# Squaring Q and K in four chunks instead of one piece, in an eight-core attention and FFN kernel

## What is computed

```python
h = layernorm(x)
Q, K, V = h @ Wq + bq, h @ Wk + bk, h @ Wv + bv          # 16 heads of 64
scores = Q K^T / sqrt(64) + mask                          # mask: -inf above the diagonal,
attn = softmax(scores)                                    #  -0.25 * log(distance) below it
x = x + (attn V) @ Wo + bo
h = layernorm(x);  hr, hi = split(h)
x = x + concat(hr Wr^T - hi Wi^T + br, hr Wi^T + hi Wr^T + bi)
```

## Time and profile before

| | us |
|---|---|
| median of 2 runs (range) | 1258.16 (1254.16 to 1262.17) |
| the profiled execution | 1259.46 |
| its span, slowest core (core 5) | 1257.9 |
| spans of the eight cores | 1235.4 to 1257.9 |
| prologue of Q, K squares on core 5 | 178.75 to 190.68 |
| attention on core 5 | 264 to 893 |

### The profile page before, as it was taken

How to read it: one execution, slowest core, us unless ns; L and a number is a source line. 1 busy time by engine, 2 the same in 40 slices (tenths; PEclk the granted TensorE clock), 3 DMA queues, 4 the chain that set the end, 5 groups by cost and what they waited for, 6 DMA issues and landing times.

```text
span 1257.9 us, 13946 instructions; the slowest of 8 cores (1235.4 to 1257.9 us)
## 1 busy us (share of the span) xinstructions
PE 767.4 (61%) x3672; PEld 263.0 (21%) x3672; DVE 603.2 (48%) x1163; ACT 451.8 (36%) x891; POOL 174.2 (14%) x132
## 2 busy tenths in 40 slices
PE   0001069695686766867669667766285746575556
PEld 0000024241221221312213122121021212121222
DVE  4555433247556475474664555545326342434342
ACT  0011010045765757667567576667300000000000
POOL 2212300014022040130350000000002010100000
PEclk9999998797796987879777789767666767768678
DMA  4111240424122031220310000000511011101101
GB/s 108 50 50 50 64 54 1 51 68 101 34 34 68 1 67 34 34 67 1 62 57 1 1 2 1 1 1 1 93 40 35 23 44 67 67 1 67 67 34 67
DMA packets 39394, 52.52 MB, mean 42 GB/s; under 512 B 21782, under 2 KB 23830, under 8 KB 39192
## 3 DMA queue, kind: packets, MB, share of 16 engines
q1 hardware_dynamic: 17944, 41.15, 9.9%
q0 software_dynamic: 21376, 10.49, 6.6%
HBM read 51.63 MB, written 8.39 MB: 48 GB/s over the span
## 4 chain that ended last, share of the span: by engine, by line
PE 47%; DVE 18%; DMA 10%; ACT 9%; issue 9%; DVEq 4%; POOL 2%; SPq 0%; ACTq 0%; POOLq 0%
PE qk L377 9%; DMA xrot<-x 7%; PE psF L938 7%; ACT PTb L630 6%; PE pv L677 6%; PE stP L605 5%; PE qk L480 5%; PE pr L692 4%; PE psW L871 4%; DVE PTb L654 3%; DVE PTb L649 3%; DVE stat L220 3%; DVEq L404 3%; POOL sqscr L218 2%; DVE stat L234 2%
## 5 line engine op out<-in xcount | busy, mean ns | idle before, releaser
L630 ACT ACTIVATE PTb<-stP,negCS 128x512 bf16<-128x512 f32 (+1 forms) x320 | 199.4, 623 | 243.8 <-PE stP L611 241.7
L649 DVE TENSOR_TENSOR PTb<-PTb,decayS 128x512 bf16<-128x512 bf16 (+1 forms) x320 | 147.0, 459 | 220.6 <-ACT PTb L630 213.4
L635 ACT ACTIVATE PTb<-stP,negCS 128x512 bf16<-128x512 f32 (+1 forms) x320 | 199.2, 622 | 0.0
L677 PE MATMUL pv<-PTb,V 128*64 128x512 bf16 (+1 forms) x320 | 138.0, 431 | 83.9 <-DVE PTb L654 78.5
L242 ACT ACTIVATE stat<-stat 128x1 f32<-128x1 f32 x32 | 6.5, 203 | 440.7 <-DVEq L237 440.6
L605 PE MATMUL stP<-QTs,KTs 64*128 64x512 bf16 (+1 forms) x320 | 133.2, 421 | 40.4 <-ACT PTb L635 40.4
L654 DVE TENSOR_TENSOR PTb<-PTb,decayS 128x512 bf16<-128x512 bf16 (+1 forms) x320 | 143.5, 448 | 16.4 <-ACT PTb L635 0.9
L685 PE MATMUL pv<-PTb,V 128*64 128x512 bf16 (+1 forms) x320 | 142.4, 445 | 0.0
L698 PE MATMUL pr<-PTb,ones 128*64 128x512 bf16 (+1 forms) x320 | 137.7, 432 | 0.0
L692 PE MATMUL pr<-PTb,ones 128*64 128x512 bf16 (+1 forms) x320 | 137.3, 431 | 0.0
L611 PE MATMUL stP<-QTs,KTs 64*128 64x512 bf16 (+1 forms) x320 | 133.8, 423 | 0.0
(11 more groups left out here) (91 smaller groups left out, 968.3 us busy)
## 6 DMA issues: line engine op xcount, KB each, us to landing
xrot<-x SPq DMA_DIRECT2D x28, 512.0 KB, 5.2
g1b<-g1rep SPq DMA_DIRECT2D x32, 256.0 KB, 2.6
g2b<-g2rep SPq DMA_DIRECT2D x32, 256.0 KB, 3.0
out<-outbuf SPq DMA_DIRECT2D x8, 1024.0 KB, 4.9
xrot<-x POOLq DMA_DIRECT2D x4, 512.0 KB, 4.3
Wqp<-wq POOLq DMA_DIRECT2D x8, 256.0 KB, 5.1
Wkp<-wk POOLq DMA_DIRECT2D x8, 256.0 KB, 6.8
WvS<-wv POOLq DMA_DIRECT2D x2, 1024.0 KB, 14.2
```

The source lines that it names most:

```text
L630: s.activation(PTb[:, slot * 1024 + no:slot * 1024 + 512], stP[j][:, no:512], AF.Exp, bias=negCS[:, pi:pi + 1]),
L635: s.activation(PTb[:, slot * 1024 + 512 + no:(slot + 1) * 1024], stP[j][:, 512 + no:1024], AF.Exp, bias=negCS[:, pi:pi + 1]),
L649: P.emit("vector", lambda v, slot=slot, off=off, no=no: v.tensor_mul(PTb[:, slot * 1024 + no:slot * 1024 + 512], PTb[:, slot * 1024 + no:s ...
L677: t.matmul(pv[0:64, no:512], V[:, mt * 1024 + h0 * 64:mt * 1024 + h0 * 64 + 64], PTb[:, slot * 1024 + no:slot * 1024 + 512], start=(mt == ...
```

## The change

Each square is cut into four of 512 columns, and each piece now stands directly in front of its own matmul and maximum, with a drain and a `yield` between square and matmul:

```diff
             for (kk, (which, srcT)) in enumerate((("q", QTs), ("k", KTs))):
-                P.emit("vector", lambda v, srcT=srcT, pi=pi: v.tensor_mul(
-                    qsqbf, srcT[:, pi * SEQ:(pi + 1) * SEQ],
-                    srcT[:, pi * SEQ:(pi + 1) * SEQ]),
-                    waits=[(aE, last_ev)])
-                sq = P.emit("vector", lambda v: v.drain(fusable=False), inc=vE)
-                yield
                 for c in range(NCH):
+                    P.emit("vector", lambda v, srcT=srcT, pi=pi, c=c: v.tensor_mul(
+                        qsqbf[:, c * 512:(c + 1) * 512],
+                        srcT[:, pi * SEQ + c * 512:pi * SEQ + (c + 1) * 512],
+                        srcT[:, pi * SEQ + c * 512:pi * SEQ + (c + 1) * 512]),
+                        waits=[(aE, last_ev)])
+                    sq = P.emit("vector", lambda v: v.drain(fusable=False), inc=vE)
+                    yield
                     j, pw = pool.acquire()
                     mm = P.emit("tensor", lambda t, j=j, c=c: t.matmul(
                         qkP[j][0:2, 0:512], hselS[:, :],
```

## The result

The changed kernel takes 1275.91 us (median of 11 runs, 1266.57 to 1288.77) against 1254.99 us before (10 runs). The ratio is 1.0153, 95% interval 1.0122 to 1.0185: slower by about 19 us. All ratios here, and the medians compared for n_before and n_after, leave out executions in the slower of the chip's two states. The forecast said 1270, +0.9%. The profiled execution took 1277.8 us. Its eight spans are longer than those of before by 24.0 us on average, the slowest one by 18.4.

What follows compares the result with a forecast made beforehand. Bound: inside a pair, a loop over PE, ACT and DVE with almost no slack. Prologue +7.7 and seven pairs +3.5 make +11.2 us on the profiled 1259.46; forecast 1270, +0.9%, range 1256 to 1286.

Steps and rivals of the forecast that it cites:

- the prologue: Before V: each cut square stands behind the previous chunk's maximum, so nothing overlaps: +7.7 us, ends +6.0 and +8.0.
- the pair's own term: Sum of the step terms in one pair, without POOL: taken as +0.5 us a pair, +3.5 us in seven.
- Steps 17 to 23: In a pair: three matmuls wait for fresh squares before attnV, 0.9 us each, +2.7 us; small chain leaves, -0.4.
- the small chain: Lines L418 to L438 in a pair: leaving steps 17 to 23 gives -0.4 us, coming to steps 25 to 28 costs 0 to +0.4.
- Steps 14 to 16: In a pair: the 2.77 us stall before K's first matmul goes; with earlier gains the pair stands at -2.7 us.
- Steps 24 to 28: End of the chunk in a pair: last matmul waits before attnV(23), +0.6 us; the small chain adds 0 to +0.4.
- POOL: In five pairs shorter but more squares meet POOL's work: bounds -0.5 to +1 us a pair, taken as 0.
- The signs: Expected in the profile: about 64 L409 waits, prologue 19 to 20 us, ACT idle about 2, every second exponential 3.9.
- A: Rival: waits with idle PE keep half clock until step 24: +3.2 us a pair, 1292 in all; chance 0.12.
- B: Rival: the clock recovers, the three attnV of step 16 run at 2.4 GHz: -1.5 us a pair, 1259; chance 0.17.
- C: Rival: the waits disappear and pairs come near pair 7's window: 49 us less in seven, 1218; chance 0.04.
- D: Rival: more short squares meet POOL: +1 us in five pairs, 1275; chance 0.67 together with the forecast.

Runs made afterwards that it cites:

- n_before: The kernel before without POOL's products, the FFN matrix set to zero once and not built: ratio 0.9761 to before, median 1223.9 us.
- n_after: The changed kernel without POOL's products, the FFN matrix set to zero once and not built: ratio 0.9891 to before, median 1242.6 us.
- e2: The kernel before with only the prologue's squares cut as in the changed kernel, the pairs keeping whole squares: ratio 1.0032.
- e1: The kernel before with only the pairs' squares cut as in the changed kernel, the prologue keeping whole squares: ratio 1.0124.
- e3: The pairs' squares cut as in the changed kernel, but each matmul three steps behind its square instead of one; prologue whole: ratio 0.9844 to before.
- e7: As e3, with cut squares in the pairs and a whole prologue, but each matmul two steps behind its square: ratio 0.9822 to before.
- e9: As e6, but each square in the pairs cut into four pieces with a drain each, all in one step: ratio 0.9937 to before.
- e6: The kernel before, whole squares, with one more empty step between each square and its first matmul: ratio 0.9785, 1229.56 us.
- e8: The kernel before, whole squares, with two more empty steps between each square and its first matmul where e6 has one: ratio 0.9861.

## Why the prediction was right, and where its sizes were off

The direction and the range held, and the mechanism was the one forecast: matmuls that wait for a square queued just behind the mask product. The size of the loss was 19 us for 11, and the two parts of the forecast were off by different amounts: the prologue was put a little too high (7.7 for 6.5 us), the pairs far too low (3.5 for 19.6). The pair's own +0.5 us was the small rest of large terms that nearly cancel, -2.7 and +2.7, so half a microsecond in any of them changes it as much as the term itself. By the prediction's own steps:

**The prologue.** Forecast +7.7 us with ends of 6.0 and 8.0; measured +6.5 in the trace, and e2 alone shows ratio 1.0032, 4 us with an interval that reaches to 8. The mechanism is as told. A chunk takes 2.09 us, not 2.19: from the start of a maximum to the end of the drain behind the next square it is 1.05 us (183.21 to 184.26 above), where I had put 0.69 + 0.03 + 0.43 = 1.15 and no overlap. The first two matmuls ran at the full clock (0.39 us).

**Steps 17 to 23.** Forecast +0.9 us for each of three waits, less 0.4 for the small chain. The exponentials of steps 17, 19, 21 and 23 start at 812.22, 816.18, 820.33 and 823.86 in pair 6 (core 3), 11.64 us in all; in the kernel before, at 790.79 and 800.10, it was 9.31. That is +2.3, as forecast, but core 3 is one of the two fortunate cores. Over the eight cores this stretch of pair 6 takes 12.3 us: 11.6 on the two with a clock of 0.98, 12.5 on the six with 0.84 or 0.85. So the forecast is right for the full clock, and the change costs up to 0.9 us more because the clock falls. The first wait, step 18, on core 3:

```profile
813.59 0.42 DVE L655 TENSOR_TENSOR PTb<-PTb,decayS 128x512 bf16<-128x512 bf16 x1
...
813.93 0.42 DVE L401 TENSOR_TENSOR qsqT<-KTs 128x512 bf16<-128x512 bf16 x1
...
814.77 0.38 PE L409 MATMUL qk<-qsqT,hselS 128*2 128x512 bf16 x1 [1.11 <-DVEq L406]
815.07 0.40 PE L678 MATMUL pv<-PTb,V 128*64 128x512 bf16 x1
...
816.18 0.69 ACT L631 ACTIVATE PTb<-stP,negCS 128x512 bf16<-128x512 f32 x1 [1.09 <-PE stP L612]
```

attnV starts 1.06 us after the mask product ended (814.01), where without the wait it is 0.14: the 0.92 that I had worked out. The same wait on core 0, where TensorE runs at the low level behind it:

```profile
812.68 0.43 DVE L655 TENSOR_TENSOR PTb<-PTb,decayS 128x512 bf16<-128x512 bf16 x1
...
813.86 0.59 PE L409 MATMUL qk<-qsqT,hselS 128*2 128x512 bf16 x1 [1.28 <-DVEq L406]
...
814.37 0.64 PE L678 MATMUL pv<-PTb,V 128*64 128x512 bf16 x1
...
816.13 0.69 ACT L631 ACTIVATE PTb<-stP,negCS 128x512 bf16<-128x512 f32 x1 [2.14 <-PE stP L612]
```

From the start of attnV to the exponential it takes 1.76 us here and 1.11 on core 3, and attnV itself starts 1.26 us after the mask product instead of 1.06. That it is the wait for a fresh square which costs most, and not the pieces, is shown by e1 against e3 and e7. The pieces are not free either: e9 against e6.

**Steps 14 to 16** were mis-sized. I let the pair stand at -2.7 us there; measured over eight cores it is -1.8 in pair 6 at the exponential of step 16 (against the kernel before, the intervals that start with the exponentials of steps 10, 11 and 15 are shorter by 0.80, 0.74 and 3.01 us, those of steps 12 and 14 longer by 0.91 and 1.85). The rows of core 3:

```profile
805.44 0.42 DVE L401 TENSOR_TENSOR qsqT<-QTs 128x512 bf16<-128x512 bf16 x1
...
806.24 0.59 PE L409 MATMUL qk<-qsqT,hselS 128*2 128x512 bf16 x1 [3.36 <-DVEq L406]
...
806.76 0.60 PE L606 MATMUL stP<-QTs,KTs 64*128 64x512 bf16 x1
...
807.30 0.63 PE L678 MATMUL pv<-PTb,V 128*64 128x512 bf16 x1
...
807.53 0.69 ACT L631 ACTIVATE PTb<-stP,negCS 128x512 bf16<-128x512 f32 x1 [1.73 <-PE stP L612]
```

PE was idle for 3.36 us in front of this matmul, more than the 2.77 of before: ACT was first busy with the reciprocals (802.08 to 803.49), and the square stands behind the mask product of step 13, whose exponentials came after them. It then ran at the half clock, so that ST(15) came 0.52 us later and attnV(12) 1.06, where I had put 0.3 and 0.5 by rows of the full clock, although showed the half clock at just this place.

**Steps 24 to 28.** Forecast +0.6 and 0 to 0.4; the means of pair 6 are +0.85 from step 24 to 25 and +0.15 over steps 26 and 27. A little low.

Together, the pair's own term was +0.5 in the forecast and is 1.9 where POOL is idle (pairs 5 and 6; n_after against n_before). The latter, over seven pairs and eight cores, by the interval that starts with the exponential of each step:

| steps | forecast | measured |
|---|---|---|
| 0 to 9 | 0 | +0.3 |
| 10 to 15 | -2.7 | -2.2 |
| 16 to 23 | +2.3 | +2.7 |
| 24 to 27 | +0.6 to +1.0 | +1.0 |
| 28 to 39 | 0 | +0.1 |

The missing 1.4 us is thus spread, most of it over the first three rows; no single row was far off. Why steps 0 to 9 are longer stays open.

**POOL** I had bounded at -0.5 to +1 a pair in five pairs and taken as 0. With POOL the seven pairs lose 6.2 us more than without, 1.2 us in each of the five. By the scatter of the cores this is uncertain by some 3 us, so it is at the upper bound and not clearly above. It is the smaller part of what is missing; the larger is the pair's own term, 7 x 1.4 = 10 us. A held-up square of 512 columns took up to 1.49 us. In those pairs the clock is low as well (0.59 in pair 3). How much is the hold-up on DVE and how much the clock was not separated.

**The signs.** ACT's idle time before the exponential of step 16 fell as told, from 4.9 to 2.0 us (pairs 5 and 6, all cores), and the prologue came near its 19. Every second exponential of steps 17 to 23 comes after 3.96, 4.15 and 3.53 us on core 3, where 3.9 was told. The waits of L409 were 56, not about 64, and longer than told: of the 48 in the pairs of core 3, 12 lie between 0.8 and 1.5 us and 28 are longer, up to 3.4 us where POOL is idle.

**The rivals.** A (half clock in steps 16 to 24) did happen, in a small way: in pair 6 on six of the eight cores, in pairs 5 and 6 of n_after in 14 of 16 cases. But by the rows of core 0 the clock fell for one of the four rounds and not for all, which costs 0.9 us where it happens instead of the 3.2 of the forecast; the price of a round, 0.66 + 0.2, was right. In pair 6 it is 0.65 us on the average of the eight cores, so over seven pairs an estimated 4 to 5 us of the loss. One of my signs, a clock well below 0.95 in these steps, thus came true, and the slowest core alone would have hidden it. B did not happen: the three attnV of step 16 still run at 0.63 us each, and PE stands idle in front of them for 3.36 us even after the change. The argument against it said so; it was not tested by itself. C did not happen with this edit. Its price was misread as well: the windows of all seven pairs lie 8.3 us above that of pair 7 on average, not 7. About half of C's 49 us can be had in another way: e6 gets 26 us out of the pairs with whole squares. D (POOL) happened at about its price, 6 us. That the result, 1276, lies at D's 1275 is luck: the pair's own term was 10 us too low, the prologue 1 us too high, the stages behind attention came out 2 us shorter, and the forecast was counted from 1259.5 where the median of before turned out as 1255.0.

## What to carry to other kernels

With in-order queues, a piece of filler that crosses engines should have its consumer behind a wait that the main loop has anyway: one more slot between producer and consumer was worth 25 us here, where cutting the producer and leaving the consumer right behind each piece lost 19. More distance is not better by itself: with a second slot (e8) 18 us of it were lost again, by the traces at the places where a matmul of Q and the small chain then stood. Ask of each consumer what stands behind it in its queue, and of each producer behind which main-loop instruction it stands; if that is the instruction for which the consumer's engine is going to wait next, the pair of them lengthens the loop by the whole hand-over, not only by the work. And price such a hand-over at the clock that TensorE has at that place, on all cores: here the slowest core kept the full clock in a stretch where six others did not.

## What was not expected of the hardware

Cutting one bf16 product of 2048 columns into four with a drain behind each makes the next product on DVE start 2.5 us after the first piece, where it started 1.48 us after the whole square: 0.61 us a piece from start to start, of which 0.42 is the piece. In seven pairs, with the queues otherwise the same, that alone was worth 1.5% of the whole kernel (0.9937 against 0.9785, e9 against e6).

The granted clock of the same stretch differs from core to core though all run the same program: in steps 16 to 24 of pair 6 it was 0.94 or 0.95 on all eight cores before the change, and after it 0.84 or 0.85 on six and 0.98 on two. On core 0 the matmul behind the first new wait (1.28 us of idle PE) takes 0.59 us; on core 3 the one behind the same wait (1.11 us) takes 0.38. No run shows what decides between the two.
